# The last segment sum of a four-layer graph network: 60 of 1616 gathered tiles are fetched row by row from SyncE's and ScalarE's queues

## What is computed

```python
h = jnp.maximum(_layernorm(x, axis=-1), 0.0)
x = x + _L3_gnn_ref(h, src, dst)
# _L3_gnn_ref(mat, row, col):
vals = jnp.take(mat, col, axis=0)
out = jax.ops.segment_sum(vals, row, num_segments=NC)
```

## Time and profile before

| what | value |
|---|---|
| median of 3 runs | 9657.09 us (9654.31 to 9661.85) |
| span of the profiled execution | 9654.6 us |
| the profiled execution's own time | not listed apart from the three runs; its span lies 2.5 us under their median |
| last sum, from its first instruction to the last addition | 7598.5 to 9636.9 us |
| last phase, to the end | 9636.9 to 9654.6 us |
| GpSimd, busy over the whole span | 6762.4 us (70%) |
| gathers of the last sum | 1616 |

### The profile page before, as it was taken

How to read it: one execution, slowest core, us unless ns; L and a number is a source line. 1 busy time by engine, 2 the same in 40 slices (tenths; PEclk the granted TensorE clock), 3 DMA queues, 4 the chain that set the end, 5 groups by cost and what they waited for, 6 DMA issues and landing times. The chain is left out here.

```text
span 9654.6 us, 111112 instructions
## 1 busy us (share of the span) xinstructions
PE 5769.7 (60%) x28659; PEld 4406.5 (46%) x28659; DVE 6268.9 (65%) x14884; ACT 2670.2 (28%) x8519; POOL 6762.4 (70%) x7106
## 2 busy tenths in 40 slices
PE   5466787778784466655666566666666244444443
PEld 2144565555554344444445455555555233333333
DVE  8999788888884566666666566666666533333333
ACT  0044111111111344444443255555555100000000
POOL 0077777777776677777776677777777577777776
PEclk6555999999997677777777899999999555555555
DMA  1000333333336433333333344444444222222224
GB/s 32 14 14 14 82 92 93 92 92 92 92 90 140 85 55 55 55 55 55 55 55 36 108 111 112 111 112 112 111 111 108 49 54 54 54 54 54 54 54 60
DMA packets 1411288, 707.04 MB, mean 73 GB/s; under 512 B 1167308, under 2 KB 1271608, under 8 KB 1410536
## 3 DMA queue, kind: packets, MB, share of 16 engines
q0 software_dynamic: 254160, 559.07, 23.1%
q1 hardware_dynamic: 1156504, 140.86, 10.4%
HBM read 595.05 MB, written 104.05 MB: 72 GB/s over the span
## 5 line engine op out<-in xcount | busy, mean ns | idle before, releaser
L1534 POOL DMA_INDIRECT l_rows<-h_tab,l_index x1616 | 1530.7, 947 | 507.5 <-issue 455.3
L650 POOL DMA_INDIRECT l_rows<-h_tab,l_words x1616 | 1524.7, 943 | 515.7 <-issue 407.5
L1151 POOL DMA_INDIRECT l_rows<-h_tab,l_index x1616 | 1526.4, 945 | 506.6 <-issue 467.2
L693 PE MATMUL l_sums<-l_onehot,l_rows 128*128 128x128 f32 x3232 | 826.9, 437 | 1294.0 <-issue 1127.6
L1669 PE MATMUL l_sums<-l_weighted,l_rows 128*128 128x256 f32 x3232 | 1186.8, 531 | 647.5 <-issue 530.8
L693 PEld LDWEIGHTS l_sums<-l_onehot,l_rows 128*128 128x128 f32 x3232 | 719.7, 328 | 1401.2 <-issue 1300.4
L681 DVE TENSOR_TENSOR acc<-acc,l_sums 128x128 f32 x1616 | 463.8, 287 | 1324.0 <-PE l_sums L693 1118.6
L1548 ACT ACTIVATE l_weighted<-l_onehot,l_weights 128x128 f32<-128x128 bf16 x3232 | 987.5, 388 | 1109.6 <-DVE l_onehot L601 1045.3
L1669 PEld LDWEIGHTS l_sums<-l_weighted,l_rows 128*128 128x128 f32 x3232 | 816.7, 265 | 816.3 <-issue 551.5
L1596 DVE TENSOR_TENSOR acc<-acc,l_sums 128x256 f32 x1616 | 678.3, 420 | 677.0 <-PE l_sums L1669 523.0
L1938 POOL DMA_INDIRECT l_kv<-kv_tab,l_words x816 | 796.8, 977 | 248.6 <-issue 248.6
(11 more groups left out here) (374 smaller groups left out, 10371.5 us busy)
## 6 DMA issues: line engine op xcount, KB each, us to landing
staged<-tmp SPq DMA_DIRECT2D x195, 304.0 KB, 2.6
l_rows<-h_tab,l_index POOLq DMA_INDIRECT x3232
l_rows<-h_tab,l_words POOLq DMA_INDIRECT x1616, 2.5
by_src<-words_src SPq DMA_DIRECT2D x96, 152.0 KB, 3.3
l_kv<-kv_tab,l_words POOLq DMA_INDIRECT x816, 2.8
l_attr<-in_edge_attr SPq DMA_DIRECT2D x44, 272.0 KB, 5.0
l_kv<-kv_tab,moments POOLq DMA_INDIRECT x600
h_tab<-h SPq DMA_DIRECT2D x21, 448.0 KB, 3.0
```

What stands on the lines that cost most here:

```text
L650: pool.indirect_dma_start(rows[b][:, j, :], None, table, bass.IndirectOffsetOnAxis(ap=words[k % 3][:, at + j, 0:1], axis=0)).then_inc(rows ...
L693: done = nc.tensor.matmul(sums[q % SUMS][:, j, 0:P], rows[b][:, j, :], onehot[b][:, j, :], start=True, stop=True)
L1151: pool.indirect_dma_start(rows[b][:, j, 0:D], None, table, bass.IndirectOffsetOnAxis(ap=index[q // Q16 % WORDS][:, q % Q16 * H + j, :], ax ...
L1534: pool.indirect_dma_start(rows[b][:, j, :], None, h_tab, bass.IndirectOffsetOnAxis(ap=index[q // Q16 % WORDS][:, q % Q16 * H + j, :], axis ...
```

## The change

Two objects of a new class `Fetcher` take one tile each in every thirteen quads (EVERY = 13) away from the gathers. SyncE's fetches the fourth tile of quads 14, 27, ..., 391; ScalarE's that of quads 20, 33, ..., 397: 30 tiles each. For one tile the engine

- loads the tile's 128 row numbers from `by_src` as one row of integers into a buffer of one partition (`load_list`, two buffers, one tile ahead);
- reads them eight at a time into registers (16 TENSOR_LOAD a tile);
- issues for each row one register instruction (number times 128 times 4 bytes) and one DMA of 512 bytes, from `h_tab` at the register's address to one partition of `fetched` (two buffers), so 128 DMAs a tile, each of which adds 16 to one semaphore.

The 16 groups of eight are dealt over thirteen quads of the engine's own program. At the start of a tile's fetch the engine waits for its list and, from the third tile on, until TensorE has used the buffer. SyncE still loads `words`, now between its groups, under the same waits. GpSimd issues three gathers in a quad with a fetched tile. TensorE waits for the gathers that are left, then for the fetched tile, and takes it as the fourth product's left side.

```diff
--- before.py
+++ after.py
@@ -51,6 +51,7 @@
 T16 = 16
 LN_EPS = 1e-5
 BINS_AHEAD = 4
+LOADS = 8
 BLOCKS = -(-DEALS // GB)
 PADDED = BLOCKS * GB + 4
 
@@ -602,6 +603,55 @@
                                    places.to_broadcast([P, tiles, P]), ALU.is_equal)
 
 
+class Fetcher:
+
+
+    def __init__(self, nc, own, engine, tag, sorted_edges, table, width, every, lag):
+        self.nc, self.engine, self.edges, self.table, self.every, self.lag = nc, engine, sorted_edges, table, every, lag
+        self.listed = [own.enter_context(nc.sbuf_tensor(f"{tag}_listed{n}", [1, P], I32)) for n in range(2)]
+        self.rows = [own.enter_context(nc.sbuf_tensor(f"{tag}_fetched{n}", [P, width], F32)) for n in range(2)]
+        self.listed_ready, self.rows_ready = ([own.enter_context(nc.semaphore(f"{tag}_{name}_ready{n}")) for n in range(2)] for name in ("listed", "fetched"))
+        self.count = (TILES // 4 - 1 - lag) // every
+
+    def quad_of(self, n):
+
+        return (n + 1) * self.every + self.lag
+
+    def number_at(self, q):
+
+        n = (q - self.lag) // self.every - 1
+        return n if 0 <= n < self.count and self.quad_of(n) == q else None
+
+    def load_list(self, eng, n):
+        t = self.quad_of(n) * 4 + 3
+        eng.dma_start(self.listed[n % 2][:], self.edges[t * P:(t + 1) * P, 0:1].rearrange("r w -> w r"),
+                      allow_slow_non_contiguous=True).then_inc(self.listed_ready[n % 2], 16)
+
+    def start(self, eng):
+        self.load_list(eng, 0)
+
+    def step(self, eng, q, used, used_by):
+
+        for unit in range(q * (P // LOADS) // self.every, (q + 1) * (P // LOADS) // self.every):
+            n, first = unit // (P // LOADS), unit % (P // LOADS) * LOADS
+            if n >= self.count:
+                return
+            if first == 0:
+                eng.wait_ge(self.listed_ready[n % 2], 16 * (n // 2 + 1))
+                if n >= 2:
+                    eng.wait_ge(used, used_by(self.quad_of(n - 2)))
+                if n + 1 < self.count:
+                    self.load_list(eng, n + 1)
+            _, rows = self.nc.values_load_multi_w_load_instructions(
+                self.listed[n % 2][0:1, first:first + LOADS], engines=(self.engine,), min_val=0, max_val=NB * P - 1,
+                skip_runtime_bounds_check_because="the sort writes row numbers below NB * P")
+            for r in range(LOADS):
+                eng.dma_start(self.rows[n % 2][first + r:first + r + 1, :], self.table[bass.ds(rows[r], 1), :]).then_inc(self.rows_ready[n % 2], 16)
+
+    def wait_rows(self, eng, n):
+        eng.wait_ge(self.rows_ready[n % 2], 16 * P * (n // 2 + 1))
+
+
 def sum_phase(nc, tag, acc, place, blk, sorted_edges, table):
 
 
@@ -625,16 +675,35 @@
 
         oh_ready, summed, added, cleared = sem("onehot_ready"), sem("pair_summed"), sem("added"), sem("cleared")
         pairs_of = lambda q: 2 * (q + 1)
+        EVERY = 13
+        by_sp = Fetcher(nc, own, ENGINE.SP, f"{tag}_sp", sorted_edges, table, D, EVERY, 1)
+        by_act = Fetcher(nc, own, ENGINE.Activation, f"{tag}_act", sorted_edges, table, D, EVERY, 1 + EVERY // 2)
+        fetchers = (by_sp, by_act)
+        fetched_at = lambda q: [(f, f.number_at(q)) for f in fetchers if f.number_at(q) is not None]
 
         with nc.Block() as block:
             @block.sync
             def _(sp):
                 blocks = tiles_of(sorted_edges, T16)
-                for k in range(TILES // T16):
+                def load_words(k):
                     if k >= 3:
 
                         sp.wait_ge(summed, pairs_of((k - 2) * Q16 - 1))
                     sp.dma_start(words[k % 3][:], blocks[k][:, :, 0:3]).then_inc(words_ready[k % 3], 16)
+
+                for k in range(2):
+                    load_words(k)
+                by_sp.start(sp)
+                for q in range(QUADS):
+                    if q % Q16 == 0 and q // Q16 + 2 < TILES // T16:
+                        load_words(q // Q16 + 2)
+                    by_sp.step(sp, q, summed, pairs_of)
+
+            @block.scalar
+            def _(act):
+                by_act.start(act)
+                for q in range(QUADS):
+                    by_act.step(act, q, summed, pairs_of)
 
             @block.gpsimd
             def _(pool):
@@ -646,7 +715,7 @@
                     if at == 0:
                         pool.wait_ge(words_ready[k % 3], 16 * (k // 3 + 1))
                     pool.nop(nofuse=True)
-                    for j in range(H):
+                    for j in range(H - len(fetched_at(q))):
                         pool.indirect_dma_start(rows[b][:, j, :], None, table,
                                                 bass.IndirectOffsetOnAxis(ap=words[k % 3][:, at + j, 0:1], axis=0)
                                                 ).then_inc(rows_ready[b], 16)
@@ -683,14 +752,20 @@
             @block.tensor
             def _(pe):
                 pe.wait_ge(cleared, 1)
+                gathered = [0] * RING
                 for q in range(QUADS):
                     b = q % RING
                     pe.wait_ge(oh_ready, q + 1)
-                    pe.wait_ge(rows_ready[b], 16 * H * (q // RING + 1))
+                    gathered[b] += H - len(fetched_at(q))
+                    pe.wait_ge(rows_ready[b], 16 * gathered[b])
+                    of = [rows[b][:, j, :] for j in range(H)]
+                    for fetcher, n in fetched_at(q):
+                        fetcher.wait_rows(pe, n)
+                        of[H - 1] = fetcher.rows[n % 2][:]
                     for j in range(H):
                         if j % 2 == 0 and q >= SUMS:
                             pe.wait_ge(added, (q - SUMS) * H + j + 2)
-                        done = nc.tensor.matmul(sums[q % SUMS][:, j, 0:P], rows[b][:, j, :], onehot[b][:, j, :],
+                        done = nc.tensor.matmul(sums[q % SUMS][:, j, 0:P], of[j], onehot[b][:, j, :],
                                                 start=True, stop=True)
                         if j % 2 == 1:
                             done.then_inc(summed, 1)
```

## The result

The changed kernel takes 9791.38 us in the median against 9657.17 us before, a ratio of 1.0138 with a 95% interval of 1.0122 to 1.0154: slower by 1.4%. The forecast was 9620 us. The time lies inside the range given (9572 to 9890) and on the other side of "no change". The median is over four executions; one of them took 13314 us, with the granted clock at 0.455 where the others had 0.77, and the ratio leaves it out.

A forecast was written before the change was run, and what follows sets the result against it. GpSimd's issue, 1.248 us a gather, was taken to bound the last sum, with SyncE becoming pacemaker at 64.3 us a tile. Span 7688 + 30 x 64.3 gives 9617, plus 2.5 for the median: 9620 us, range 9572 to 9890.

The forecast's parts named there:

- What bounds the sum before: Last sum: GpSimd's issue sets the pace at 1.248 us a gather; only the last few gathers are bound by data.
- SyncE becomes the pacemaker: Last sum: a fetched tile costs SyncE 64.3 us to issue, against 62.4 us of gathers in thirteen quads.
- A row: SyncE's issue of one row: transfer 275 ns, register instruction 46, two gaps of 43; 407 ns, 52.1 us a tile.
- The register load: SyncE reading eight row numbers into registers: 598 ns plus 43, sixteen times, 10.3 us a tile.
- Words and list: SyncE's other loads a tile: 3.25 loads of words, 1.3 us, and one list, 0.6 us.
- theory C: Posed for the experiments: queue order, a late list or words behind rows, keeps SyncE waiting; no size given.
- What this makes of the end: End of the last sum: span = 7688 + 30 P, P being SyncE's time for a tile; 9617 for P = 64.3.
- Rival 1: SyncE's transfer of a row at 265 ns or less: full gain, GpSimd stays the bound, 9581 us; chance 0.26.
- Rival 2: SyncE's rows cannot start sooner than 475 ns apart: 73.0 us a tile, median 9881 us; chance 0.25.
- Rival 3: SyncE's transfer of 432 ns with the register instruction behind it: 564 ns a row, 10223 us; chance 0.12.
- Rival 4: SyncE and ScalarE take turns at one generator, each row holding it 455 to 475 ns: 11230 us; chance 0.05.
- The one more write: SyncE's one-row transfers: remaining semaphore counts written by the sequencer, 17 + 43 ns, would make P 72.0, median 9850.

The follow-up runs named there:

- load_once_c: Changed kernel with one register load a tile instead of sixteen, fetching the same eight rows sixteen times: 9605.18 us against 9675.91 for the kernel before, ratio 0.9927.
- every15_c: Changed kernel with one tile in every fifteen quads instead of thirteen on both engines: 9613.82 us against 9675.91 for the kernel before, ratio 0.9937.
- mixed: Changed kernel with SyncE taking one tile in fifteen quads and ScalarE one in fourteen, 54 tiles: 9606.14 us against 9668.17 for the kernel before, ratio 0.9935.
- both16: Changed kernel with sixteen numbers a register load, SyncE one tile in fourteen quads, ScalarE one in thirteen: 9606.44 us against 9674.41 for the kernel before, ratio 0.9929.
- loads16_b: Changed kernel with sixteen numbers a register load instead of eight: 9717.49 us, ratio 1.0042 to the kernel before.
- sp_only_c: Changed kernel with only SyncE fetching, ScalarE's thirty tiles gathered by GpSimd again: 9800.43 us, ratio 1.0129 to the kernel before.
- every15_b: Changed kernel with one tile in every fifteen quads, run where the kernel before takes 11400 to 11600 us: 12570.54 us, ratio 1.0871.

## Why the prediction was wrong

By its own steps:

- **What bounds the sum before** held. With SyncE under the gathers' time (load_once_c, every15_c) the gathers come at their old pace, and the time saved falls short of the removed gathers' number times 1.248 us by 3 to 5 us (medians, with mixed and both16).
- **SyncE becomes the pacemaker** held, but not "by a hair". The step that failed is the sum of a tile's issue time: 64.3 us forecast, 70.0 measured. 5.7 us times 30 is 171 us, the whole of the miss (9791 - 9620). Added up over the trace, from each instruction of SyncE to the next, a tile is 13.4 us of register loads (10.3 forecast), 54.4 of rows (52.1) and 2.2 of words and lists (1.9): 3.2, 2.3 and 0.2 us too little. Either of the first two alone would have carried the sum over 65.6, where by the prediction's own rule the gain is gone.
- **A row** was right in the median, 407 ns forecast and 410 measured, by parts that weren't: the transfer takes 228 ns and not 275, the register instruction 37 and not 46, and there is a second one, a MOVE of 29 ns with its gap, which the order of instructions doesn't list and which I had not counted. The errors cancel there, which is luck. On average a row takes 425 ns: the first one behind a register load takes 450 in the median, the six after it 411, and single steps are longer.
- **The register load** is the term that was mis-sized most. I took VectorE's 598 ns for eight numbers as SyncE's; SyncE's takes 788 (ScalarE's 830). 16 x (0.788 + 0.03) = 13.1 us, against 10.3: 2.8 us a tile, 84 us of the 171. I scaled the register instruction down by the ratio of the two engines' semaphore instructions and left the load as it was; the load goes the other way. The first load of a tile takes 975 ns, the others 787, which makes it 13.4 on average. It was dearer than any register load of the trace before, and the range given (350 to 598) had no upper side. loads16_b, which changes the loads alone, confirms that they are on the path; load_once_c doesn't separate them from the register instructions.
- **Words and list**: 3.25 x (0.40 + 0.04) + 0.52 + 0.04 = 2.0 us against 1.9.
- With 128 x 0.41 = 52.5 these come to 67.6 us. The remaining 2.4 us a tile lie in steps longer than the median: 1.9 in rows, 0.3 in loads, 0.2 in lists, by the sums above. One of them is a wait in the queue, as theory C has it: once, in the first tile, SyncE stands over 5 us before a load of words, where the program waits for `summed`. It is worth 0.2 us a tile.
- **What this makes of the end**: 2 + 63.5 + 17.7 = 83.2 us from the last row's issue to the end of the span, measured 9787.2 - 9703.9 = 83.3, and 83.7 in loads16_b. With P = 70.0 the rule gives 9788. This part of the prediction was right.
- **ScalarE** needs (9652.0 - 7603.5) / 30 = 68.3 us a tile, its waits for a free buffer included, and stays off the path, as said. Its row is cheaper (transfer 213 ns), its load dearer.
- **Rival 1** (full gain) asked for a transfer of 265 ns or less; the transfer is below that, and the gain didn't come, because the condition was put on one term while another had moved. **Rival 2** gave a time close to the measured one (9727 to 9881) by a mechanism that is not there: rows stand 410 ns apart, not 475. That the measured time lies in its stretch is luck. The argument set against it, that the thirteen transfers have 128 pieces each, was also misread: one of them (`w_we`) has 16 partitions, 8 KB, and takes 429 ns like the others (line below), so 16 pieces are no cheaper there than 128. **Rival 3** falls with it. **Rival 4**, the generator that two engines share: transfers take 224 to 228 ns on SyncE with ScalarE's rows beside them and without (sp_only_c), and ScalarE's 213. By the rule of the Trainium skill (Perfetto Trace Analysis, "DMA Instruction — HWDGE (DVE, Sync)") a lock would show in just this duration. It does not show even where the records of the two engines overlap (232.0 ns against 231.9), so if there is a lock, it holds nobody up by an amount that these rows show.
- The one more write for transfers on fewer than 16 engines (the Trainium skill, DMA: Bandwidth & Descriptors, "Why a DMA increments its semaphore by 16 and not by 1") does not show as a cost: the transfer of one row is the cheapest of all that SyncE issued, 224 ns at the least against 303. Whether the write happens, no run here shows.

```profile
L1396 SPq DMA_DIRECT2D w_we<-in_L_gnn_We x1: 429/429/429, 3196.2 to 3196.2; - x1
```

The sum lay within a few per cent of the balance, where each 10 ns of a row is 38 us and each 100 ns of a load 48 us. The chances reflected that (0.48 faster, 0.40 slower). The point took every price from another engine or another form of transfer, and had nothing added for what such rows leave out: an instruction not listed, and steps longer than the median.

## What to carry to other kernels

When an idle queue takes over work by many small steps, compare its issue time a round with the bound engine's time a round. Here being 12% over (70.0 us against 62.4) turned a gain of 0.7% into a loss of 1.4%. So plan the share with slack (here one tile in fifteen quads instead of thirteen): a tile given up forgoes 1.25 us, while a tile that takes 7.6 us too long costs nearly that each of thirty times. Price each instruction of such a step on the engine that will issue it, the register loads above all, and leave the estimate open upward where only another engine's row is at hand.

## What the runs showed of the hardware that was not expected

- A register load costs SyncE 788 ns for eight numbers and 1248 for sixteen in the median (a straight line through the two has 328 fixed and 57.5 each). The first load of a tile takes 975, and the only one left in load_once_c 976, so the count does not say it all. ScalarE's takes 830 for eight; VectorE's, in the kernel before, 598 for eight and 350 for four.
- The transfer of one 512-byte row with its address in a register takes SyncE 228 ns and ScalarE 213, less than any transfer of the kernel before (303), and the whole row 0.41 us with its two register instructions.
- Two queues issuing 256 such rows in 70 us do not slow each other measurably: 70.0 us a tile against 69.8 alone, and 232.0 ns for the transfers that overlap one of the other queue against 231.9 for the rest.
- Beside six runs the kernel before took 18 to 20% longer than beside the others, and there SyncE's queue of many short instructions was stretched by 74% (every15_b against every15_c). The cause is open.
